# Strassen's seven products for fc1 over pairs of token tiles, with weights split at each use

## The reference

```python
h = gelu(x @ fc1_w.T + fc1_b)                       # 512 -> 2048
x = x + concat(h @ fc2_w.T + fc2_b,                 # 2048 -> 384
               h @ experts_w[indices].T + be)       # 2048 -> 128, one expert a sequence
x = x + x @ weight[subject_id].T + b                # "l1", 512 -> 512, by sequence
x = x + L2(x)   # gates, four causal traces, three 512 x 512 products, a layer norm
x = x + x @ weight3[ids] + b3                       # "l3", by sequence
```

## Time and profile before

| | us |
|---|---|
| median of 3 runs (lowest, highest) | 1357.03 (1356.0, 1357.3) |
| the profiled execution, its own time | 1356.39 |
| its span in the trace | 1354.7 |
| PE busy in it | 1348.4 |
| DVE busy, ACT busy | 785.7, 492.3 |

### The profile page before, as it was taken

The page is one execution under the profiler, slowest core; times in us unless marked ns, Lnnn a source line. Parts: engine busy times, 40 slices in busy tenths (PEclk is TensorE's granted clock), DMA queues, the critical chain, the costliest instruction groups (busy, mean ns, idle before and its releaser), DMA issues.

```text
span 1354.7 us, 15221 instructions
## 1 busy us (share of the span) xinstructions
PE 1348.4 (100%) x5917; PEld 1108.8 (82%) x5917; DVE 785.7 (58%) x1047; ACT 492.3 (36%) x816; POOL 119.6 (9%) x155
## 2 busy tenths in 40 slices
PE   9999999999999999999999999999999999999998
PEld 7888888888888888888887887878888888888877
DVE  4335243332252332341321486999999989998985
ACT  5444233332242332341421222243525252525254
POOL 5000100000100000100000222003100310031000
PEclk9999999999999999999999999999999999999999
DMA  5523433503532502530412955731232123212101
GB/s 134 140 70 116 123 111 120 160 4 114 140 117 86 155 33 84 163 113 25 135 67 74 218 155 174 200 94 63 94 125 94 62 94 125 94 62 92 48 16 63
DMA packets 69480, 140.90 MB, mean 104 GB/s; under 512 B 7408, under 2 KB 19696, under 8 KB 66464
## 3 DMA queue, kind: packets, MB, share of 16 engines
q1 hardware_dynamic: 61456, 116.71, 27.8%
q0 software_dynamic: 6176, 16.88, 4.4%
q10 hardware_dynamic: 1776, 6.34, 1.4%
HBM read 86.85 MB, written 53.05 MB: 103 GB/s over the span
## 4 chain that ended last, share of the span: by engine, by line
PE 90%; DVE 7%; issue 1%; ACT 1%; DMA 0%; SPq 0%; DVEq 0%
PE bank L1088 30%; PE bank L1089 30%; PE bank L1090 30%; DVE drive L1555 2%; DVE drive L1540 1%; DVE temporal L1565 1%; DVE temporal L1555 1%; DVE bank L1516 0%; DMA x_raw<-in_x 0%; DVE spikes_lo L1399 0%; DVE temporal_lo L1399 0%; DVE sumsq L1613 0%; DVE rstd L1621 0%; DVE gated L1524 0%; DVE soma L1600 0%
## 5 line engine op out<-in xcount | busy, mean ns | idle before, releaser
L1399 DVE TENSOR_TENSOR h_hl<-bank,h_hl 128x512 fp32r<-128x512 f32 x128 | 88.6, 692 | 468.1 <-ACT h_hl L944 468.1
L1088 PE MATMUL bank<-x_hl,wa 128*128 128x512 f32 x512 | 199.7, 390 | 0.5 <-DVE x_hl L1399 0.4
L1089 PE MATMUL bank<-x_hl,wa 128*128 128x512 f32 x512 | 199.2, 389 | 0.0
L1090 PE MATMUL bank<-x_hl,wa 128*128 128x512 f32 x512 | 199.2, 389 | 0.0
L1088 PE MATMUL bank<-h_hl,wa 128*128 128x512 f32 x512 | 199.2, 389 | 0.0
L1089 PE MATMUL bank<-h_hl,wa 128*128 128x512 f32 x512 | 199.2, 389 | 0.0
L1090 PE MATMUL bank<-h_hl,wa 128*128 128x512 f32 x512 | 199.2, 389 | 0.0
L940 ACT ACTIVATE bank<-bank,small_sb 128x512 f32<-128x512 f32 x128 | 84.2, 658 | 212.4 <-PE bank L1090 212.2
L944 ACT ACTIVATE h_hl<-bank 128x512 fp32r<-128x512 f32 x128 | 76.7, 599 | 230.4 <-PE bank L1090 229.9
L1088 PEld LDWEIGHTS bank<-x_hl,wa 128*128 128x128 f32 x512 | 96.0, 188 | 22.6 <-DVE x_hl L1399 1.4
L1088 PEld LDWEIGHTS bank<-h_hl,wa 128*128 128x128 f32 x512 | 96.2, 188 | 20.0
(11 more groups left out here) (197 smaller groups left out, 2318.7 us busy)
## 6 DMA issues: line engine op xcount, KB each, us to landing
x2hl_dram<-x_hl POOLq DMA_DIRECT2D x28, 512.0 KB, 9.0
x_slot<-x2hl_dram SPq DMA_DIRECT2D x26, 513.0 KB, 4.5
stage<-in_l_w SPq DMA_DIRECT2D x32, 256.0 KB, 3.1
x_dram<-x_raw SPq DMA_DIRECT2D x8, 1024.0 KB, 5.6
xt<-x_dram SPq DMA_DIRECT2D x8, 1024.0 KB, 5.9
x_raw<-in_x SPq DMA_DIRECT2D x7, 1024.0 KB, 8.4
out<-y_sb SPq DMA_DIRECT2D x28, 256.0 KB, 2.3
l3w_hl<-l3w_dram SPq DMA_DIRECT2D x12, 512.0 KB, 7.8
```

The source lines that it names most:

```text
L1088: eng.matmul(ps, w_hi, x_hi, start=first, stop=False)
L1089: eng.matmul(ps, w_hi, x_lo, start=False, stop=False)
L1090: return eng.matmul(ps, w_lo, x_hi, start=False, stop=final)
L1399: return eng.tensor_tensor(lo, raw, hi.bitcast(F32), ALU.subtract)
```

## The change

fc1 is done for the two tiles of a sequence together (a pair, `p` = 0 to 3). Weights of two hidden blocks (`2k`, `2k + 1`) and the two halves of the 512 features form a 2 x 2 matrix A; the halves of the features and the two tiles form B. Instead of 8 products of quarters, seven are made, P1 to P7, of A's quarters or sums of them and B's quarters or sums (T1 to T4). One product is 2 chunks x 3 = 6 matmuls. The results are C11 and C21 (the first tile's two blocks of `h`) and C12 and C22 (the second's):

- P1 is copied to SBUF by ACT (`p1_of`). P2 is added to it in PSUM: C11.
- U2 = P6 + P1 (`u2_of`, DVE). P7 is added to P6 in PSUM, and U3 = that + P1 (`u3_of`).
- C22 = P5 + U3 (`c22_of`). P3 is added to P5 in PSUM, and C12 = that + U2 (`c12_of`). C21 = U3 - P4 (`c21_of`).

C11 and C21 go on to gelu, the split and fc2 as before. C22 and C12 get their gelu in SBUF and are stored to `hb_dram`; after the 8 units `k` of a pair, the 16 blocks of the second tile come back (`load_hb`), are split, and run through fc2 alone. I call the 8 units the first phase of a pair, and the 16 blocks `j` that follow its second phase.

The resident `wa` is gone. The seven operands of a unit's weights are split one unit ahead into a ring of 8 (`product_hi`, `product_lo`), and every fc2 block at each use (`w2_hi`, `w2_lo`, ring of 3). POOL makes the four sums of weights of each unit (`sums_of`, one buffer), and for pairs 1 to 3 the four sums of B (`parts_of`); for pair 0 DVE does that. Pair 0 has its own start: P1 and P2 of four units, three blocks of fc2, then the other products. Parked weights come up to two a unit, and l1 of a second tile stands in unit 1 of the next pair.

```diff
-        wa = place("wa", 0, [HC, 2, NB, P], F32R)
...
-            for u in range(UNITS + 2):
-                t, j = divmod(u, HC)
-                if u < UNITS:
-                    fc1(u)
-                if u >= 2:
-                    fc2(u - 2)
...
+        ORDER = ("P1", "P6", "P5", "P2", "P7", "P4", "P3")
+        FIRST_ORDER = ("P6", "P5", "P4", "P7", "P3")
+        PRODUCTS = [(0, k, "P1") for k in range(4)] + [(0, k, "P2") for k in range(4)]
+        PRODUCTS += [(0, k, x) for k in range(4) for x in FIRST_ORDER]
+        PRODUCTS += [(p, k, x) for p in range(PAIRS) for k in range(K8) for x in ORDER if p or k >= 4]
...
+            parked_here = ((0, 0, 0, 0, 1, 1, 1, 2), (0, 2, 2, 2, 2, 2, 2, 2), (0, 2, 2, 2, 2, 2, 2, 2),
+                           (0, 1, 1, 1, 1, 0, 0, 0))[p][k]
...
+            load_raw_first(0)
+            load_part_a(0, 0)
+            load_part_a(0, 1)
+            for k in range(1, 4):
+                load_raw_first(k)
+            load_part_a(0, 2)
+            load_part_a(0, 3)
+            load_w2(0)
...
+            load_exp(0, 0)
+            load_part_b(0, 0)
+            load_part_b(0, 1)
+            load_part_c(0, 0)
+            load_part_c(0, 1)
+            load_w2(1)
+            load_exp(0, 1)
+            load_raw(0)
+            load_raw(1)
+            load_w2(2)
+            load_exp(0, 2)
+            load_w2(3)
...
+                for j in range(HC):
+                    load_hb(p, j)
+                    if 1 <= j < 5:
+                        load_part_a(p + 1, j - 1)
+                    if j in (5, 6):
+                        load_part_b(p + 1, j - 5)
+                    if j in (7, 8):
+                        load_part_c(p + 1, j - 7)
...
+            def sums_of(p, k):
+                r = K8 * p + k
+                raw = fc1_raw[r % 2]
+                on.wait_ge(s_raw[r % 2], 16 * (r // 2 + 1))
+                if r:
+                    on.wait_ge(s_slo, prod_no(*divmod(r - 1, K8), "P3") + 1)
+                a11, a12 = raw[:, 0, 0:HALF, :], raw[:, 0, HALF:KC, :]
+                a21, a22 = raw[:, 1, 0:HALF, :], raw[:, 1, HALF:KC, :]
+                s1, s3, s2, s4 = [s_raw_sb[:, s, :, :] for s in range(4)]
+                eng.tensor_tensor(s1, a21, a22, ALU.add).then_inc(s_smade, 1)
+                eng.tensor_tensor(s3, a11, a21, ALU.subtract).then_inc(s_smade, 1)
+                on.wait_ge(s_smade, 4 * r + 1)
+                eng.tensor_tensor(s2, s1, a11, ALU.subtract).then_inc(s_smade, 1)
+                on.wait_ge(s_smade, 4 * r + 3)
+                eng.tensor_tensor(s4, a12, s2, ALU.subtract).then_inc(s_smade, 1)
...
+            def parts_of(p):
+                on.wait_ge(s_txb, 32 * (p + 1))
+                on.wait_ge(s_txc, 32 * (p + 1))
+                b21, b22, t1, t2, t3, t4 = [t_raw[:, b, :, :] for b in (T4, B22, T1, T2, T3, T4)]
+                b12, b11 = t1, t2
+                eng.tensor_tensor(t3, b22, b12, ALU.subtract).then_inc(s_tmade, 1)
+                on.wait_ge(s_tmade, 4 * p + 1)
+                eng.tensor_tensor(t1, b12, b11, ALU.subtract).then_inc(s_tmade, 1)
+                on.wait_ge(s_tmade, 4 * p + 2)
+                eng.tensor_tensor(t2, b22, t1, ALU.subtract).then_inc(s_tmade, 1)
+                on.wait_ge(s_tmade, 4 * p + 3)
+                eng.tensor_tensor(t4, t2, b21, ALU.subtract).then_inc(s_tmade, 1)
+
+            sums_of(0, 0)
+            sums_of(0, 1)
             on.wait_ge(s_idx, 32)
...
+            def product_hi(n):
+                p, k, x = PRODUCTS[n]
+                r = K8 * p + k
+                if x in SUM:
+                    on.wait_ge(s_smade, 4 * r + SUM[x] + 1)
+                elif p or k >= 4 or x == "P4":
+                    on.wait_ge(s_raw[r % 2], 16 * (r // 2 + 1))
...
+            for k in range(4):
+                p1_of(0, k)
+                if k < 3:
+                    w2_hi(k)
+            h_of_c11(0, 0)
+            h_of_c11(0, 1)
+            h_of_c11(0, 2)
+            part_hi(0, T2, 0)
+            part_hi(0, T2, 1)
+            part_hi(0, T1, 0)
+            part_hi(0, T1, 1)
+            h_of_c11(0, 3)
...
+                    hb_hi(v)
+                    w2_hi(v)
+                    if j in (2, 3):
+                        x1_hi(t, 2 * (j - 2))
+                        x1_hi(t, 2 * (j - 2) + 1)
+                    if j in (9, 10):
+                        x2_hi(t, 2 * (j - 9))
+                        x2_hi(t, 2 * (j - 9) + 1)
+                    if p < PAIRS - 1:
+                        for at, part in zip((4, 5, 6, 7, 11, 12, 13), T_ORDER):
+                            if j == at:
+                                part_hi(p + 1, part, 0)
+                                part_hi(p + 1, part, 1)
+                        continue
...
+                    product(p, k, "P1")
+                    product(p, k, "P6")
+                    product(p, k, "P5")
+                    product(p, k, "P2")
+                    product(p, k, "P7")
+                    if p == 0 and k < 6:
+                        fc2(3 + k)
+                    elif k == 2:
+                        fc2(v - 4)
+                        fc2(v - 3)
+                    elif k > 2:
+                        fc2(v - 3)
+                    product(p, k, "P4")
+                    if k == 1:
+                        for m in range(KC):
+                            l1(HALVES * p - 1, m)
+                    elif k >= 2 and (p or k >= 6):
+                        fc2(v - 2)
+                    product(p, k, "P3")
+                for v in range(13, HC):
+                    fc2(2 * HC * p + v)
+                for j in range(HC):
...
+            def c12_of(p, k):
+                e = K8 * p + k
+                on.wait_ge(s_prod, prod_no(p, k, "P3") + 1)
+                on.wait_ge(s_hbst[0], 16 * e)
+                eng.tensor_tensor(hb_out[0][:, :], product_banks(p)[2][:, :], u2_sb[:, :], ALU.add
...
+            def unit(p, k):
+                ahead, uses = next_products(p, k), w2_in_unit(p, k)
+                if k != 1:
+                    c12_of(p, k - 1)
+                for n in ahead[0:1]:
+                    product_lo(n)
+                u2_of(p, k)
+                for n in ahead[1:3]:
+                    product_lo(n)
+                w2_lo(uses[0])
+                for n in ahead[3:4]:
+                    product_lo(n)
+                h_lo_c11(p, k)
+                u3_of(p, k)
+                c22_of(p, k)
+                for n in ahead[4:5]:
+                    product_lo(n)
+                if k == 2 and p:
+                    for c in range(KC):
+                        x2_lo(HALVES * p - 1, c)
+                if p == 0 and k == 6:
+                    constants()
+                staged_lo(p, k)
+                for n in ahead[5:6]:
+                    product_lo(n)
+                for v in uses[1:]:
+                    w2_lo(v)
+                c21_of(p, k)
+                h_lo_c21(p, k)
+                for n in ahead[6:7]:
+                    product_lo(n)
```

1056 lines of the change are left out of this document (682 added, 374 removed).

## The result

The changed kernel takes 1542.28 us (median of 4 runs, 1539.57 to 1551.19) against 1356.82 before; the ratio is 1.138, with a 95% interval of 1.133 to 1.143. The forecast was 1391. The sign was right and the size was not: 185.5 us slower where 34 were expected.

The account below looks back on a forecast made before the run. The prediction took the first stage to be bound by PE's count of matmuls. Losses of 77.1 us less a gain of 43.3 made net +33.8, so 1391 us by the median, with an 8-in-10 range of 1364 to 1422.

Parts of the forecast that it names:

- What bounds the kernel: First stage: bound by PE's count of matmuls; fewer give time back only while the three engines feeding PE keep pace.
- Start: Pair 0's start: PE waits for loads, in-order ACT and DVE lists and POOL's list before unit 1's P3; loss 33.8 us.
- Units 4 and 5: Pair 0, units with one fc2: PE's 12.2 us against a DVE loop of 13.5; loss 2.5 us in all.
- first units: First unit of pairs 1 to 3: P3 waits for c22_of, the next P2 for its P1 copy; loss 7.0 us.
- B for the next pair: Second phases: PE waits for POOL's four late sums of B and what follows them; 12 us in three pairs.
- Units with two parked pieces: Pairs 1 and 2: P5 waits for the bank that c12_of empties, behind the pieces' splits and store; loss 15.6 us.
- Case 3: Buffers absorb the waits put on c12_of and block 7; start, first units and C12's return remain: 1364, chance 0.11.
- First block from DRAM: After P3 of unit 7: C12's gelu, load and splits outlast three fc2 blocks where c12_of(7) is late; loss 5.2 us.
- Tail: Entry to the second stage: DVE has about 9 us more to do, mostly taken up; loss 1 us, loads nothing.
- Rival 2: POOL is held up by DVE, its sums taking 1.2 for 256 and 3.0 for 1024: 1413, chance 0.17.
- Rival 1: PE's clock falls in new gaps, eight matmuls at half clock after each of four: 7 us, 1398, chance 0.25.
- criteria at the forecast's end: Prediction wrong if POOL's sums run far from 0.6 and 2.1, start gaps are missing, or unlisted gaps exceed 10 us.

Follow-up runs that it names:

- pool_order: Changed kernel with POOL's index reads and bias loads ahead of the sums of units 0 and 1, zero stores behind those of units 3 to 6: 1527.61 us.
- experiment 2: Changed kernel with the chunks of split x2 stored apart and the 1 MB copy of x2 behind the last load of h: 1511.63 us.
- experiment 5: Changed kernel with the second parked piece, and the l1 piece behind it, split at the unit's end, same work in each unit: 1507.12 us.
- experiment 6: Changed kernel with only the table of parked pieces changed: one, not two, in units 2 to 4 of pairs 1 and 2, more in pair 3: 1493.51 us.
- the last kernel: all_moved plus three moves, the first h load ahead of unit 7's late piece, x2's chunks and the parts' splits further apart: 1382.13 us.
- 11: all_moved plus odd tile's x2 split over two units, first h load ahead of the C12 store, three DVE operations ahead of last x1 sums: 1404.66 us.
- all_moved: Changed kernel with POOL's start reordered, x2 transfers apart, parts' splits later, pieces spread, the second late, fc2 loads first: 1403.46 us.

## Why the prediction was wrong

- *What bounds the kernel* and the gain were right: 192 matmuls less, and the three feeding engines' lists decide.
- *Start* (33.8): measured 27.3. Both gaps came at their places, 6.8 at 18 us and 15.9 at 60, behind the named lists, and pool_order took the second away. The third fc2 split began at 24.2 and not 28, so the first gap is shorter, and the matmuls at half clock behind both are counted in their own row. (The load list adds up to 6.4 MB and not 6.3, which moves nothing.)
- *Units 4 and 5*, *first units*, *B for the next pair*: within 2 us each (2.0, 6, 13.6). The last is in part luck: its bounds allowed 1.5 to 23, and in pair 0 the sums took 1.2 more than the middle taken, what follows them 0.9 less. The step that read POOL's fourth sum against block 7 gave 4.0 a pair and the trace has 4.1 to 4.8.
- *Units with two parked pieces* (15.6, measured 77 with pair 3's 7.6) is the step that failed most. It walked DVE's loop with compute rows and took one landing, the store of `stage_hi`, at its quiet 2.0; "an l1 piece 0.6 more" counted its split and not its load. Two things were left out. SP's serial list: store, wait for the low part's landing, load the next item, 3.4 until it is there; in unit 3 of pair 1 ACT stands 3.4 for the store and 3.5 for the load. And the neighbours: in unit 2 the store takes 9.9. The waits of 4 us and more stood exactly in the units with two parked and an l1 piece; behind unit 6, with two parked alone, PE stood 0.9 in pair 2, where the sum had 1.3, and not at all in pair 1. Experiments 2 and 5 each took out tens of microseconds with no pass less in these units, so the rival *work* cannot explain what they took out. 13.3 and 13.2 remained in the two units 2 after experiment 5, 10.2 and 9.8 after experiment 2; they went only in experiment 6 and with all moves together, where these units have a piece less to split as well. Whether it is what remains (20.0 us in 13 waits for `c12_of` in the last kernel) was not tried.
- *Case 3*, that the buffers absorb the loop, is refuted, and so is its end of the range, 1364. (The three terms that it keeps, 46.0, give 1360; with the 2.5 of units 4 and 5 and the tail's 1 it is 1363.)
- *First block from DRAM* (5.2, measured 10.7; by pair 0.2, 3.0, 2.0, 0 against 4.3, 2.9, 2.3, 0.9): pairs 1 and 2 are right and pair 0 is the miss. There the longest wait, 2.6, is for a split of fc2 weights that stands in ACT's list behind the gelu of the C12 block, so what came late is `c12_of(7)` more than the load. SP's list was as empty as assumed: the load left 0.4 us behind that gelu and landed after 2.9 (3.3 and 4.2 in pairs 1 and 2). It became the limit only in the kernels with late pieces, where one stands in front of it (the chain in 11).
- *Late waits of the second phase* (29.0): not in the forecast. The sum asked what the loads of B meet, and never what x2's 2.1 MB and its 1 MB copy do to loads of `h`, which leave only some 8 us ahead of their use. Before, PE's waits were tenths of a microsecond.
- *Tail* (1, measured 7.5): the step that failed is "the loads of the second stage (wg, slots) have 25 us and more: nothing". It left out the load of `mod_t`, for which DVE stood 10.3 us. DVE's backlog of 9 us, on which the term was built, was mostly taken up as I had assumed: PE's last l1 product ended at 1011.9 and DVE took it at 1014.4, 2.5 us late. The late loads of `h` are not the cause, since all_moved, without them, has the same 10.3 and 7.5. In the next two kernels, with three of DVE's operations (2.1 us) moved ahead of the last x1 sums, DVE's wait is 8.3 and 8.0 and PE's 4.9 and 4.6.
- *POOL*: 0.6 a sum of 256 was 0.74 alone and 0.88 on average; 2.1 was 2.39. Rival 2's mechanism, waiting for DVE, cost little: the sums of 1024 took 2.39 with little scatter.
- *Rival 1, the clock*, was right in its mechanism, at 34 to 38 us and not 7. The sum had it at nothing, and the rival gave it only the four gaps of my own sum. There are 20 waits of 3 us and more, and 6 to 13 matmuls at 0.43 stand behind all but one of them, 1.2 to 2.8 us. The other 16 to 20 us of that row nobody had in the forecast: they are what 48 more stops add to the busy time that the trace shows. Filling the waits of one pair with products gave 6.0 us.
- Of the criteria at the forecast's end, the last one held: gaps of a kind not listed held more than 10 us, 29.0 in the second phases, and the half clock besides.

## What to carry to other kernels

When a kernel gets its first waits for transfers in an in-order list, price each landing by what else is on the DMA engines then, not by its row in a quiet kernel: here 2.0 became 9.9 and 3.1 became 14.5. Walk the queue's own list as carefully as an engine's: store, wait for landing, load, landing is one chain, and a load that nobody counts as waiting can stand behind it. Do so for the loads at the start of the next stage as well: the 10.3 us wait for `mod_t` was in no list. And when PE was never idle before, add to each new wait of some microseconds the slow matmuls behind it. Saving 3% of the matmuls did not carry all this here, even with most waits gone (1382 against 1357).

## What was unexpected in the hardware

- PE's slow stretch behind a wait is short and does not grow with the wait: 12 matmuls and 2.5 us lost behind 17.5 us, 13 and 2.7 behind 5.5, 6 and 1.3 behind 7.6.
- A 256 KB store beside a burst of another queue took 9.9 us with 2.1 MB in the burst and 8.2 with 4.2 MB.
- A halo store of 1 KB landed after 14.4 us. While x2 and its halo leave, the DMA engines are mostly over 90% busy and move mostly 115 to 300 GB/s, where just before they reach 360 to 497; 336 packets are under 512 bytes. Which kind of packet costs it was not separated. The DMA view of the changed kernel, 205 to 235 us, busy tenths and GB/s in 40 slices:

```profile
DMA  0074550004498999599989979998995999799300
GB/s 0 22 191 155 172 166 15 0 0 22 147 497 360 470 393 382 137 340 232 134 121 153 118 145 270 200 115 137 156 202 131 238 153 229 131 289 300 96 0 0
DMA packets 3153, 5.26 MB, mean 175 GB/s; under 512 B 336, under 2 KB 1872, under 8 KB 3024
...
x2hl_dram<-x_hl POOLq DMA_DIRECT2D x4, 1.0 KB, 14.4
```
